# Turning the mixed spectra on VectorE instead of through DRAM, in a frequency-domain token mixer

## The reference, cut to what matters

```python
Vf = jnp.fft.rfft(phi, n=n, axis=0)                 # n = 4096, 16 filters
Uf_p = jnp.fft.rfft(u, n=n, axis=1)                 # u: (images, tokens, 64)
Uf_m = jnp.fft.rfft(u * sgn3, n=n, axis=1)          # alternating signs
U_plus = jnp.fft.irfft(Vf[None, :, :, None] * Uf_p[:, :, None, :], n=n, axis=1)[:, :sl]
U_minus = jnp.fft.irfft(Vf[None, :, :, None] * Uf_m[:, :, None, :], n=n, axis=1)[:, :sl]
U_minus = U_minus * sgn[None, :, None, None]
out = jnp.einsum('btkd,k,kde->bte', U_plus, s, Mpp)
out = out + jnp.einsum('btkd,k,kde->bte', U_minus, s, Mpm)
```

## Time and profile before

| | |
|---|---|
| time, median of three runs | 1475.58 us (1473.2 to 1476.07) |
| the profiled execution's own time | 1476.14 us |
| span of the profiled execution | 1474.5 us |
| PE busy | 1257.3 us (85%) |
| DVE busy | 985.8 us (67%) |
| ACT busy | 822.3 us (56%) |
| POOL busy | 502.7 us (34%) |
| moved by DMA | 317.66 MB |

### The profile page before, as it was taken

One profiled execution on the slowest core, in us unless ns is written; L12 is line 12 of the kernel. 1 busy time (PEld: TensorE's weight loads), 2 busy tenths in 40 slices (PEclk: granted clock), 3 DMA queues, 4 the chain that ended last, 5 costly groups with the idle time before them and its releaser, 6 DMA issues. The chain is left out here.

```text
span 1474.5 us, 37538 instructions
## 1 busy us (share of the span) xinstructions
PE 1257.3 (85%) x15089; PEld 887.7 (60%) x15089; DVE 985.8 (67%) x1420; ACT 822.3 (56%) x1487; POOL 502.7 (34%) x441
## 2 busy tenths in 40 slices
PE   1899999999999965988899999999999954965657
PEld 1455555555555532278799899899989932433334
DVE  5288888888888888765577677667767732532234
ACT  1787877888787742554466565556655521322223
POOL 2145566665566665101222223232222231000000
PEclk9999999999999986589999999999999986988778
DMA  7024455455455365328999889888889868978883
GB/s 222 1 88 145 153 190 180 145 155 184 152 180 193 106 150 172 126 82 237 271 285 289 259 255 277 240 243 267 259 255 260 250 185 314 408 309 341 332 327 131
DMA packets 179624, 317.66 MB, mean 215 GB/s; under 512 B 14805, under 2 KB 154423, under 8 KB 162935
## 3 DMA queue, kind: packets, MB, share of 16 engines
q1 hardware_dynamic: 164966, 257.47, 56.4%
q0 software_dynamic: 14592, 59.26, 11.1%
HBM read 162.93 MB, written 153.76 MB: 215 GB/s over the span
## 5 line engine op out<-in xcount | busy, mean ns | idle before, releaser
L1020 POOL DMA_DIRECT2D w_scratch<-wf x256 | 151.3, 595 | 467.5 <-ACT y_sb L1198 432.4
L1079 PE MATMUL ring<-v_mov,m_sta 105*128 105x128 f16 x4096 | 234.0, 219 | 0.0
L1079 PEld LDWEIGHTS ring<-v_mov,m_sta 105*128 105x128 f16 x4096 | 231.5, 98 | 0.4
L1215 DVE COPY hf<-ring 128x512 f32<-128x512 f32 x256 | 168.7, 689 | 26.8 <-PE ring L1079 25.8
L1198 ACT ACTIVATE hf<-ring 128x512 f32<-128x512 f32 x256 | 153.0, 598 | 58.7 <-PE ring L1079 56.7
L491 POOL TENSOR_TENSOR u_t<-u_t,root 98x1024 f32<-98x1024 f32 x62 | 118.1, 1936 | 169.7 <-DVE root L799 169.7
L535 PE MATMUL ring_norm<-x_all,center 128*128 128x448 f32 (+2 forms) x384 | 148.8, 513 | 25.0 <-PEq L211 15.7
L1404 ACT ACTIVATE out_sb<-p_turn 128x392 f32<-128x392 f32 x128 | 62.6, 498 | 189.2 <-PE p_turn L1360 174.6
L1348 PE MATMUL p_out<-w_in,last_masked 128*98 128x512 f32 x256 | 140.0, 631 | 23.9 <-DMA w_in<-w_scratch 23.9
L1393 DVE TENSOR_TENSOR x_in<-p_out,x_in 98x512 f32<-98x512 f32 x96 | 65.3, 690 | 123.0 <-DMA x_in<-x_scratch 70.0
L594 PE MATMUL ring_norm<-u_t,step_masked 98*128 98x512 f32 x256 | 126.8, 624 | 22.0 <-POOL u_t L491 22.0
(11 more groups left out here) (133 smaller groups left out, 1958.3 us busy)
## 6 DMA issues: line engine op xcount, KB each, us to landing
z_in<-z_scratch SPq DMA_DIRECT2D x32, 1076.5 KB, 8.4
z_scratch<-z_sb SPq DMA_DIRECT2D x16, 2048.0 KB, 8.9
y_scratch<-y_sb SPq DMA_DIRECT2D x32, 1024.0 KB, 9.0
yt<-y_scratch SPq DMA_DIRECT2D x64, 512.0 KB, 6.3
w_scratch<-wf POOLq DMA_DIRECT2D x256, 128.0 KB, 5.3
w_in<-w_scratch SPq DMA_DIRECT2D x8, 4096.0 KB, 16.2
x_all<-in_x SPq DMA_DIRECT2D x16, 1568.0 KB, 7.6
x_scratch<-x_t SPq DMA_DIRECT2D x16, 1568.0 KB
```

Of the source, the lines that this page charges most:

```text
L1020: nc.gpsimd.dma_start(w_units[u, h, s, c], wf[64 * c:64 * c + 64, 2 * h + s].rearrange("p (g n) -> p g n", n=256)).then_inc(w_stored, 16)
L1079: mm = nc.tensor.matmul(bank[:, 2 * NF * i:2 * NF * i + 2 * NF], m_sta[:, 2 * e + 1 - n:2 * e + 3 - n, :].rearrange("k b d -> k (b d)"), v ...
L1215: return nc.vector.tensor_copy(dst, src)
```

## The change

The trip through `y_scratch` is taken out. When all four "mix" chunks of a unit are ready, VectorE turns them with four instructions that transpose blocks of 32 x 32, straight from the four PSUM banks into `yt`, 16 output channels at a time. For that the frequencies are dealt to the banks and column tiles in another order. `yt` has one buffer, `y_sb` none. VectorE copies seven of the 16 "h" chunks now instead of eight, and ACT nine; ACT copies no "mix" chunk. The inverse is done for the unit just before (`LAG_INV` = 1), with eight matmuls of 64 rows x 64 columns instead of sixteen of 32 x 64, none of which accumulates, and its moving operand is read with a step of 32 elements. SP's queue keeps the loads of `z_in`, `fwd` and `inv` (half as large), all behind the wait for "x" chunk 3.

```diff
+    inv = inv.transpose(0, 1, 4, 2, 3, 5).reshape(NUNIT, 4, 16, 2, 2 * NA)
+    inv = inv.transpose(0, 1, 3, 2, 4).reshape(NUNIT, 128, 2 * NA)
...
-LAG_INV = 2
+LAG_INV = 1
 RING = 7
+H_ON_VECTOR = (1, 3, 5, 8, 10, 12, 14)
+def owner(stage, k):
+    if stage == "mix":
+        return 1
+    return int(k in H_ON_VECTOR) if stage == "h" else k % 2
...
             def body(u, slot, use):
+                sp.wait_ge(chunk_ready, chunks_until(u, pos["x", 3]))
+                after_wait(sp, sp_turn)
                 if not known(u, NUNIT - 2, NUNIT - 1):
                     load(u + 2, slot)
-                for e in range(2):
-                    sp.wait_ge(saved[e], chunks_until(u, pos["mix", 3], e))
-                store_y(slot)
                 if not known(u, 0, 1):
                     load_inv(u, slot)
-                sp.wait_ge(y_stored[slot], 16 * use)
-                load_y(slot)
...
+            stage, k, _ = chunks[at]
+            last = pos["mix", 3] if stage == "mix" else at
+            eng.wait_ge(saved[owner(stage, k)], chunks_until(w, last, owner(stage, k)))
...
-                                f = 16 * k + 4 * i + j
+                                f = 16 * j + 4 * k + i
...
-                        pe.wait_ge(y_loaded[slot], 32 * (use - 1))
-                        pe.wait_ge(inv_loaded[slot], 16 * (use - 1))
-                        for c in range(2):
-                            for r in range(2):
-                                for n in range(4):
...
+                        pe.wait_ge(saved[1], chunks_until(u - 1, pos["mix", 3], 1))
+                        pe.wait_ge(inv_loaded[1 - slot], 16 * (use if slot else use - 1))
+                        for h in range(2):
+                            for c, row in ((0, 0), (1, 1), (1, 0), (0, 1)):
+                                images = slice(16 * h + 8 * c, 16 * h + 8 * c + 8)
+                                rows = slice(64 * row, 64 * row + 64)
+                                mm = nc.tensor.matmul(
+                                    ring[64 * c:64 * c + 64, pos["inv", 2 * h + row] % RING, :],
+                                    inv[1 - slot][rows, :], yt[rows].rearrange("p e i -> p i e")[:, images, :],
+                                    start=True, stop=True, tile_position=(64 * row, 64 * c))
+                                if c != row:
+                                    mm.then_inc(chunk_ready, 1)
...
-                    eng.wait_ge(chunk_ready, chunks_until(u, p))
+                    eng.wait_ge(chunk_ready, chunks_until(u, pos["mix", 3] if stage == "mix" else p))
...
-                        copy(y_sb[slot][:, 4 * k:4 * k + 4, :].rearrange("p i n -> p (i n)"), bank
-                             ).then_inc(saved[which], 1)
+                        e = slice(16 * k, 16 * k + 16)
+                        nc.vector.transpose(
+                            yt[:, e, :], ring[:, first_mix:first_mix + 4, :]
+                            .rearrange("p b (i r e) -> p e r (b i)", r=2, e=CH)[:, e]).then_inc(saved[which], 1)
```

More of the change, by code:

```diff
@@ L896, in chunks_until @@
     plan = unit_chunks()
+    mine = [(stage, at) for stage, k, at in plan if engine in (None, owner(stage, k))]
     if isinstance(u, int):
[L898 to L902, removed]
+        return sum(1 for w in range(u + 1) for stage, at in mine
+                   if chunk_is_there(stage, w) and (w < u or at <= p))
+    missing = LAG_INV * sum(1 for stage, at in mine if stage in TAIL)
+    return len(mine) * u - missing + sum(1 for stage, at in mine if at <= p)
 def mix_frequencies(nc, d, keep):
@@ L909, in mix_frequencies @@
     NCH = len(chunks)
-    assert NCH % RING == 0 and NCH % 2 == 0
+    assert NCH % RING == 0
     pos = {(s, k): p for s, k, p in chunks}
+    first_mix = pos["mix", 0] % RING
+    assert first_mix + 4 <= RING
     with ExitStack() as own:
@@ L920, in mix_frequencies @@
         fwd = [sb(f"fwd{i}", [128, 3 * NF]) for i in range(2)]
-        inv = [sb(f"inv{i}", [128, 2, 2 * NA]) for i in range(2)]
+        inv = [sb(f"inv{i}", [128, 2 * NA]) for i in range(2)]
         xf = sb("xf", [128, NF, NIMG])
         hf = sb("hf", [128, NF, 2, CH])
-        y_sb = [sb(f"y_sb{i}", [128, NF // 4, 2 * CH]) for i in range(2)]
-        yt = [sb(f"yt{i}", [128, NIMG // 2, 2, CH]) for i in range(2)]
+        yt = sb("yt", [128, CH, NIMG])
         wf = sb("wf", [128, 4, 8 * CH])
@@ L937, in mix_frequencies @@
         inv_loaded = [sem(f"inv_loaded{i}") for i in range(2)]
-        y_stored = [sem(f"y_stored{i}") for i in range(2)]
-        y_loaded = [sem(f"y_loaded{i}") for i in range(2)]
         chunk_ready, v_ready, v_saved, w_stored, w_free = (
             sem(n) for n in ("chunk_ready", "v_ready", "v_saved", "w_stored", "w_free"))
-        sp_turn, pool_turn = sem("sp_turn"), sem("pool_turn")
+        sp_turn, pool_turn, pe_turn = sem("sp_turn"), sem("pool_turn"), sem("pe_turn")
         m_ready, m_zeroed, v_high, scaled, scale_step, reals_done = (
@@ L1037, in bank_free @@
                 w, at = (u, p - RING) if p >= RING else (u - 1, p - RING + NCH)
[L1038 to L1042, removed]
+            else:
+                before = [(w, at) for w in range(u + 1) for stage, _, at in chunks
+                          if chunk_is_there(stage, w) and at % RING == p % RING and (w < u or at < p)]
+                if not before:
+                    return
                 w, at = before[-1]
-                eng.wait_ge(saved[at % 2], chunks_until(w, at, at % 2))
+            stage, k, _ = chunks[at]
+            last = pos["mix", 3] if stage == "mix" else at
+            eng.wait_ge(saved[owner(stage, k)], chunks_until(w, last, owner(stage, k)))
         def all_saved(eng, u, p):
@@ L1099, in unit @@
                             bank_free(pe, u, pos["inv", at])
-                        pe.wait_ge(y_loaded[slot], 32 * (use - 1))
-                        pe.wait_ge(inv_loaded[slot], 16 * (use - 1))
-                        for c in range(2):
-                            for r in range(2):
-                                for n in range(4):
[L1105 to L1111, removed]
+                        pe.wait_ge(saved[1], chunks_until(u - 1, pos["mix", 3], 1))
+                        pe.wait_ge(inv_loaded[1 - slot], 16 * (use if slot else use - 1))
+                        after_wait(pe, pe_turn)
+                        for h in range(2):
[8 more added lines that the diff above has]
+                                    mm.then_inc(chunk_ready, 1)
                     if stage != "inv":
@@ L1115, in body @@
             def body(u, slot, use):
-                unit(u, slot, use, True, not known(u, 0, 1))
+                unit(u, slot, use, True, not known(u, 0))
             for c in range(M_CHUNKS):
@@ L1131, in _ @@
             two_by_two(pe, NUNIT, body)
-            for u in (NUNIT, NUNIT + 1):
-                unit(u, u % 2, u // 2 + 1, False, True)
+            unit(NUNIT, NUNIT % 2, NUNIT // 2 + 1, False, True)
         def m_part(c):
@@ L1140, in saver @@
         def saver(eng, which, copy):
-            mine = [(stage, k) for stage, k, p in chunks if p % 2 == which]
+            mine = [(stage, k) for stage, k, p in chunks if owner(stage, k) == which]
             first_inv = min(k for stage, k in mine if stage == "inv")
-            first_mix = min(k for stage, k in mine if stage == "mix")
             last_h = max(k for stage, k in mine if stage == "h")
@@ L1156, in unit @@
                 for stage, k, p in chunks:
-                    if p % 2 != which or not (tail if stage in TAIL else head):
+                    if owner(stage, k) != which or not (tail if stage in TAIL else head):
                         continue
-                    eng.wait_ge(chunk_ready, chunks_until(u, p))
+                    eng.wait_ge(chunk_ready, chunks_until(u, pos["mix", 3] if stage == "mix" else p))
                     bank = ring[:, p % RING, :]
                     if (stage, k) == ("inv", first_inv):
-                        eng.wait_ge(w_free, u - 1)
-                    if (stage, k) == ("mix", first_mix) and not known(u, 0, 1):
-                        eng.wait_ge(y_stored[slot], 16 * (use - 1))
+                        eng.wait_ge(w_free, u)
                     if stage == "x":
@@ L1207, in _ @@
             unit = saver(act, 0, copy)
-            two_by_two(act, NUNIT, lambda u, slot, use: unit(u, slot, use, True, not known(u, 0, 1)))
-            for u in (NUNIT, NUNIT + 1):
-                unit(u, u % 2, u // 2 + 1, False, True)
+            two_by_two(act, NUNIT, lambda u, slot, use: unit(u, slot, use, True, not known(u, 0)))
+            unit(NUNIT, NUNIT % 2, NUNIT // 2 + 1, False, True)
         @block.vector
@@ L1246, in _ @@
             unit = saver(dve, 1, copy)
-            two_by_two(dve, NUNIT, lambda u, slot, use: unit(u, slot, use, True, not known(u, 0, 1)))
-            for u in (NUNIT, NUNIT + 1):
-                unit(u, u % 2, u // 2 + 1, False, True)
```

(2 more changed lines are left out.)

16 lines of the change are left out of this document (1 added, 15 removed).

## The result

| | before | after |
|---|---|---|
| median | 1475.8 us (4 runs, 1473.2 to 1480.1) | 1505.0 us (4 runs, 1501.4 to 1511.9) |
| ratio | | 1.021 (95% interval 1.018 to 1.023) |
| profiled execution, span | 1474.5 us | 1504.7 us |

A forecast was written before the change was run, and what follows sets the result against it. PE was taken to set the pace, at 16.78 us per steady unit. Added VectorE wait +15.5, long units -13.0 and stage end -12.2 sum to -9.7, giving 1466 us beside 1475.6; range 1452 to 1500.

The forecast's parts named there:

- PE's own work: v, x, h and mix are the same matmuls; the inverse keeps four records in a row per tile, costed at nothing.
- rival (b): Inverse's moving operand, read with a 128-byte step, is slow: about +1.8 us per inverse, 1523; a third, 1485; chance 0.15.
- The tiles: In the inverse, four 64x64 tiles work at once, two of them on the same rows, as in the convolution.
- The transposes: Four on VectorE after each mix, taken as 0.64 us apart, near the 0.604 of copies from PSUM.
- The wait in "h": PE waits at h chunk 6 for the bank of x 3: 0.50 us per unit, +15.5 over 31 units.
- The long units: Units near the start and 16 to 18: of 19.8 us beyond steady units 6.8 stay, so -13.0.
- the "issue" gap: A 3.48 us gap in unit 2's mix, with no profiled cause that the change removes, so it stays.
- the wait on the w store: Units 3 and 4: inverse copies waited 9.81 us for POOL's store; x1 issued earlier takes the +9.7 away.
- (c): Waits only move: store of w meets x1 in another unit, GpSimd's standstill costs the same; -5, 1474; chance 0.15.
- GpSimd's standstill: Units 16 to 18: GpSimd stood still 6.17 us amid its DMAs; the units' +6.1 is taken away.
- The end of the stage: From the last mix to the next stage's first load: 19.8 us in place of 32.0, so -12.2.
- The 9.64 taken for a store: End of the stage: POOL's store, eight DMAs without y beside them, takes 9.64 us where it took 11.36.

## Why the prediction was wrong

The forecast was 1466 in a range of 1452 to 1500; the kernel takes 1505. Point by point:

- **PE's own work, costed at nothing: this failed.** The forecast said that no row shows the step of the moving operand, and the sum then took zero for it. It is 1.64 us in each of 31 units, 51 us in all. It was rival (b), for which I had worked out about 1.8 us in a unit, and gave 0.15, half of that to a partial case. The direction and nearly the size were on paper; the weight was wrong.
- **The evidence against (b) did not bear on it.** The 178 ns of the loads side by side are a mean over stretches at different granted clocks (0.81 from 1300 to 1400); at a granted clock of 0.98 (groups by form, 1250 to 1300) they are as long as the strided ones:

```profile
L1348 PEld LDWEIGHTS p_out<-w_in,last_masked 128*98 128x98 f32 x66 | 8.3, 166 | 0.0
```

The loads as such do escape the cost: 320 of them, overlapping, fill 36.0 us, 0.112 us for each, where 98 columns at the inverse's 0.86 us for 512 would be 0.165 (an estimate). So the row was sound for weight loads and said nothing on the moving operand; why the two differ is open. The Trainium skill's rule that spoke for (b) ("Advanced Engine Details and Errata", Memory Cachelines) is about accesses to SBUF and names no engine, and a step of 128 bytes falls under it; it should have weighed more than a row of another instruction.
- **The tiles: right.** Four 64x64 tiles at once, as the convolution suggested: 602 ns a record.
- **The transposes: right, within 0.03 us.** Assumed 0.64 apart; measured 2.51 less 0.685, over 3: 0.61.
- **The wait in "h": right in place, large by 0.30 us.** Forecast 0.50 in each unit, measured 0.20: 0.03 x 4 from the transposes, the `v_mov` instructions and `xf` copies overlap (904.36 to 905.10, 0.74 in place of 0.86), and the copies take 3.48 instead of 3.52. In sum +6 instead of +15.5.
- **The long units: the sum right by luck (6.8 forecast, 6.7 measured), its parts not.** I kept the "issue" gap and dropped the wait on the w store. The store wait stayed (10.13 us on ScalarE), moved with `x1` into unit 2, as (c) had it; and the gap shrank from 3.48 to 1.32 us. GpSimd's standstill costs nothing now, as forecast: it is 3.33 us instead of the 6.17 that the forecast kept, and each DMA of the store lands in a median of 2.6 us instead of 5.3.
- **The end of the stage: -12.2 forecast, -14.3 measured.** The 9.64 taken for a store runs from its first DMA to SP's load behind it; its last DMA lands after 6.8. So the store begun at 1235.14 has landed when the copies start at 1242.18, and they wait for PE alone.

With the inverse at its real price the same steps would have given 1466 + 51 = 1517; the 12 us to the measured 1505 are the 9 of the wait in "h" and the 2 of the end. The range ended at 1500 although the whole of (b) was worked out at 1523: that case was left outside on the strength of the weight loads.

## What to carry to other kernels

When a copy is removed by letting TensorE read a tile in another order, look at the innermost step of its moving operand first: float32 elements 16 bytes or more apart took up to twice the time here (0.86 us for a round of 512 columns at a step of 128 bytes in place of 0.43). Put the reordering where PSUM is read, since copies out of PSUM took steps of 32 bytes at no cost here, on VectorE and ScalarE. And before a large load is issued early, see which small store, waited for by the pace-setting engine, will be on the way beside it.

## What the runs showed of the hardware

- TensorE's moving operand in float32: 602, 621, 850, 1079 and 1036 ns for a record of 512 columns at steps of 4, 8, 12, 16 and 128 bytes. At 128 bytes it is the same in tiles of 32 rows (1034) and of 64 rows (1036), and with one column tile on a set of rows (1035) or two.
- That cost does not go with PE's clock: sixteen records with the step take 3.64 us at a granted clock of 1.00 and 3.67 at 0.54; without it 1.95 and 3.52.
- Strided weight loads do not pay it: 320 loads of 98 float32 columns with a step of 128 bytes fill 36.0 us, 0.112 us for each, and one lasts 165 ns; loads of neighbouring columns last 166 ns at a granted clock of 0.98.
- VectorE's 32x32-block transpose of 128x512 float32, read from four PSUM banks with a step of 512 bytes: 685 ns, 0.61 us apart, as a copy. Written with a step of 256 bytes: 1040 ns.
- Eight DMAs of 128 KB issued by GpSimd took 24 us beside 6.3 MB of loads in flight and 6.7 to 6.9 in most other units of the same kernel (10.6 and 13.9 where GpSimd stood still); with the trip through DRAM they took mostly 10 to 13. PE had a gap in its instruction stream beside those loads (3.48 us before, 1.32 after), which went when the loads were moved away.
- GpSimd stood still for 3.3 to 6.2 us ahead of the 114th and for 3.6 us ahead of the 227th of the 256 DMAs that it issued in this stage, in all thirteen kernels.
